# Attention outputs kept feature-major into the output projection, in a two-layer-norm FFN, attention, FFN kernel on one core

## The reference

```python
x = x + 0.5 * ffn(layernorm(x))          # FP4 quantise-dequantise in blocks of 16, gate/up 256 -> 704, down 704 -> 256
x = x + attn(layernorm(x), w_qkv, w_out)
x = x + 0.5 * ffn(layernorm(x))

def attn(x, w_qkv, w_out):               # 16 heads of 16 features
    q, k, v = split(einsum('bte,fe->btf', x, w_qkv))
    weights = softmax(einsum('bihd,bjhd->bhij', q, k) * 16 ** -0.5)
    attn = einsum('bhij,bjhd->bhid', weights, v)
    return einsum('btf,ef->bte', concat(attn over heads), w_out)
```

## Time and profile before

| | |
|---|---|
| median of 3 runs | 4236.52 us (4235.23 to 4238.32) |
| the profiled execution, own time | 4238.47 us |
| span of the profiled execution | 4236.7 us |
| TensorE clock granted, mean | 0.984 |
| busy: PE, DVE, ACT, POOL | 4088.2, 3740.0, 2465.5, 1089.6 us |

### The profile page before, as it was taken

The page is one execution under the profiler, slowest core; times in us unless marked ns, Lnnn a source line. Parts: engine busy times, 40 slices in busy tenths (PEclk is TensorE's granted clock), DMA queues, the critical chain, the costliest instruction groups (busy, mean ns, idle before and its releaser), DMA issues. The chain is left out here.

```text
span 4236.7 us, 109983 instructions
## 1 busy us (share of the span) xinstructions
PE 4088.2 (96%) x46770; PEld 2148.8 (51%) x46770; DVE 3740.0 (88%) x6453; ACT 2465.5 (58%) x2780; POOL 1089.6 (26%) x1190
## 2 busy tenths in 40 slices
PE   3999989889999999999999999999999999899999
PEld 2777765534444444444444444444444443677776
DVE  7999973679999999999999999999999995599998
ACT  1222225457777777777777777777777777222222
POOL 3888863300000000000000000000000000388886
PEclk7999999989999999999999999999999999999999
DMA  2000003300000000000000000000000000000000
GB/s 110 1 1 1 1 1 116 130 24 25 17 24 18 24 18 23 19 22 19 21 21 21 22 19 23 18 24 17 25 17 25 17 25 2 0 11 16 21 16 20
DMA packets 53392, 103.23 MB, mean 24 GB/s; under 512 B 10800, under 2 KB 37808, under 8 KB 52400
## 3 DMA queue, kind: packets, MB, share of 16 engines
q1 hardware_dynamic: 52912, 96.30, 6.8%
HBM read 61.93 MB, written 33.55 MB: 23 GB/s over the span
## 5 line engine op out<-in xcount | busy, mean ns | idle before, releaser
L881 DVE TENSOR_REDUCE mx<-ps_b 128x1 f32<-128x512 f32 x4032 | 2495.8, 682 | 109.8 <-PE ps_b L953 16.9
L868 ACT ACTIVATE probs<-ps_s 128x1024 f32<-128x1024 f32 x2048 | 1984.0, 1021 | 730.1 <-PE ps_s L1000 730.1
L953 PE MATMUL ps_b<-K,Q 96*32 96x512 bf16 x16128 | 1594.3, 381 | 15.5 <-DMA K<-qk_parts_dram 14.0
L1000 PE MATMUL ps_s<-Q,K 99*32 99x512 bf16 x16384 | 1429.0, 379 | 2.4 <-ACT probs L868 2.4
L978 PE MATMUL ps_o<-probs,V 128*32 128x512 f32 x8192 | 1062.3, 591 | 0.4 <-ACT probs L868 0.4
L1000 PEld LDWEIGHTS ps_s<-Q,K 99*32 99x32 bf16 x16384 | 455.2, 97 | 624.8 <-issue 283.8
L953 PEld LDWEIGHTS ps_b<-K,Q 96*32 96x32 bf16 x16128 | 444.7, 96 | 639.0 <-issue 264.7
L499 PE MATMUL ps_gu_f<-w_guT,zT_f 128*128 128x352 f32 x2048 | 635.6, 464 | 10.4 <-DVE h_f L404 9.5
L827 POOL TENSOR_TENSOR neg_parts<-neg_max,zeros 128x16 bf16<-128x16 f32 x64 | 14.2, 222 | 1892.8 <-issue 1793.0
L499 PEld LDWEIGHTS ps_gu_f<-w_guT,zT_f 128*128 128x128 f32 x2048 | 383.3, 192 | 205.4 <-ACT zT_f L356 12.0
L509 PE MATMUL ps_dn_f<-w_dnT,hT_f 128*128 128x256 f32 x1536 | 353.0, 379 | 5.3 <-ACT hT_f L361 5.3
(11 more groups left out here) (116 smaller groups left out, 2624.4 us busy)
## 6 DMA issues: line engine op xcount, KB each, us to landing
qk_parts_dram<-qk_parts SPq DMA_DIRECT2D x96, 256.0 KB, 2.8
Q<-qk_parts_dram SPq DMA_DIRECT2D x64, 192.0 KB
K<-qk_parts_dram SPq DMA_DIRECT2D x64, 192.0 KB
x_res<-in_L_attn_x SPq DMA_DIRECT2D x4, 2048.0 KB, 19.4
Q<-qk_parts_dram SPq DMA_DIRECT2D x64, 128.0 KB
K<-qk_parts_dram SPq DMA_DIRECT2D x64, 128.0 KB
out<-x_res SPq DMA_DIRECT2D x16, 512.0 KB, 2.6
Q<-qk_parts_dram SPq DMA_DIRECT2D x64, 64.0 KB
```

What stands on the lines that cost most here:

```text
L868: nc.scalar.activation(probs[:, (2 * kt + half) % 4, :], ps_s[:, half, :], ACT.Exp, scale=float(DH) ** -0.5).then_inc(exped, 1)
L881: nc.vector.tensor_reduce(mx[:, s, k // 4, bass.ds(k % 4, 1)], ps_b[:, bank, :], AX.X, ALU.max).then_inc(bank_free, 1)
L953: last = nc.tensor.matmul(ps_b[j:j + STRIP, bank, :], Q[s][0:PAIRS, qt * P + j:qt * P + j + STRIP], K[s][0:PAIRS, kb * 512:(kb + 1) * 512] ...
L1000: last = nc.tensor.matmul(ps_s[j:j + STRIP, half, (c % 2) * 512:(c % 2 + 1) * 512], K[s][:, kt * P + j:kt * P + j + STRIP], Q[s][:, c * 51 ...
```

## The change

The output tile `OT` is no longer transposed. After each head SP issues eight DMAs (`store_head`): for each of the four column groups one moves the 16 feature rows to their place in a feature-major array (16 partitions of a group of eight heads, 2048 tokens along the row; the first group into a buffer of its own, group `n` over the V of group `n-1`), and one moves the denominator row, four partitions of 128, into `denom`. After each eighth head (`g % 8 == 0`), DVE inverts the 128x128 denominators at `kt == 6`, and SP stores them to DRAM, waits for that, and issues eight DMAs which each broadcast one head's 2048 inverses over 16 partitions of `factor` (`spread_denominators`). In the next head POOL multiplies the group's 128x2048 outputs by `factor` in four instructions (`scale_group`). The eighth group is finished inside `merge_phase`. The ring has 65 fills per head. ACT's wait before its copy to `OT` is now for the moves of the head before (`out_moved`).

`merge_phase` multiplies the feature-major arrays as the stationary operand directly with `w_outT`, in 32 groups of two tiles over eight PSUM banks; its last eight groups (batch 3) wait for the last scaling. To make room, the FFN weights are stored to DRAM during the first FFN, their SBUF space holds Q and K of slots 1 and 2 during attention, and SP loads them back in `merge_phase`; the V slots lie in the space of `w_qkvT`.

```diff
+GROUP = P // DH
+OUT_MOVES = 8
...
+    def group(self, n):
+        return self.first_group[:] if n == 0 else self.va[:, (n - 1) * S:n * S]
+def store_head(sp, m, g):
+    n, h = g // GROUP, g % GROUP
+    rows = m.group(n)
+    for c in range(4):
+        sp.dma_start(rows[h * DH:(h + 1) * DH, c * 512:(c + 1) * 512], m.OT[32 * c:32 * c + DH, :]).then_inc(m.out_moved, 16)
+        sp.dma_start(m.denom[h * DH + 4 * c:h * DH + 4 * (c + 1), :],
+                     m.OT[32 * c + DH:32 * c + DH + 1, :].rearrange("o (j q) -> o j q", q=P)).then_inc(m.out_moved, 16)
+def spread_denominators(sp, m, n):
+    sp.wait_ge(m.denom_inverted, n + 1)
+    sp.dma_start(m.denom_home.rearrange("h (p q) -> (h p) q", q=P), m.denom[:]).then_inc(m.denom_stored, 16)
+    sp.wait_ge(m.denom_stored, 16 * (n + 1))
+    if n > 0:
+        sp.wait_ge(m.out_scaled, 4 * n)
+    for h in range(GROUP):
+        sp.dma_start(m.factor[h * DH:(h + 1) * DH, :], m.denom_home[h:h + 1, :].broadcast_to([DH, S])).then_inc(m.factor_loaded, 16)
+def invert_denominators(nc, dve, m, n):
+    dve.wait_ge(m.out_moved, (n + 1) * GROUP * OUT_MOVES * 16)
+    nc.vector.reciprocal(m.denom[:], m.denom[:]).then_inc(m.denom_inverted, 1)
+def scale_group(nc, pool, m, n):
+    rows = m.group(n)
+    pool.wait_ge(m.factor_loaded, (n + 1) * GROUP * 16)
+    for c in range(4):
+        part = rows[:, c * 512:(c + 1) * 512]
+        nc.gpsimd.tensor_tensor(part, part, m.factor[:, c * 512:(c + 1) * 512], ALU.mult).then_inc(m.out_scaled, 1)
...
+            @block.sync
+            def _(sp):
+                if out is None:
+                    sp.dma_start(m.w_ffn_home, m.w_ffn[:]).then_inc(stored, 16)
+                    sp.wait_ge(stored, 16)
+                else:
...
-    FILLS = UNITS + 2
+    FILLS = UNITS + 1
     MAX_AT = 11
     NEG_AT = 13
-    OUT_AT = 3
+    INVERT_AT = 6
...
+        slots = m.w_ffn[0:ROWS, :].bitcast(BF16)
+        Q = [m.Q0[:]] + [slots[:, (2 * s - 2) * S:(2 * s - 1) * S] for s in range(1, SLOTS)]
+        K = [m.K0[:]] + [slots[:, (2 * s - 1) * S:2 * s * S] for s in range(1, SLOTS)]
+        V = [m.w_qkvT[:].rearrange("p k f -> p (k f)").rearrange("p (s t c) -> p s t c", s=SLOTS, c=32)[:, s] for s in range(SLOTS)]
...
+                    if known(g, 1):
+                        sp.wait_ge(o_kept, g)
+                        store_head(sp, m, g - 1)
+                    if known(g, 1) and g % GROUP == 0:
+                        spread_denominators(sp, m, g // GROUP - 1)
...
+                    if g > 1 and g % GROUP == 1:
+                        scale_group(nc, pool, m, g // GROUP - 1)
...
-                        act.wait_ge(inv_done, g - 1)
-                    nc.scalar.copy(OT[:], ps_o[:]).then_inc(o_kept, 1)
+                        act.wait_ge(m.out_moved, (g - 1) * OUT_MOVES * 16)
+                    nc.scalar.copy(m.OT[:], ps_o[:]).then_inc(o_kept, 1)
...
-                def normalise(ring, g):
-                    at, bank = ring.next()
-                    o = ps_b[:, bank].rearrange("p (j c d) -> p j c d", j=4, c=4)
-                    dve.wait_ge(bank_full, at + 1)
-                    dve.wait_ge(bank_free, at)
-                    nc.vector.reciprocal(denom[:], o[:, :, :, DH]).then_inc(inv_done, 1)
-                    dve.wait_ge(inv_done, g)
-                    to = m.va.rearrange("p (g c j d) -> p g j c d", c=4, j=4, d=DH)
-                    nc.vector.tensor_tensor(to[:, g - 1], o[:, :, :, 0:DH],
-                                            denom[:].unsqueeze(3).broadcast_to([P, 4, 4, DH]), ALU.mult).then_inc(bank_free, 1)
...
-                        if kt == OUT_AT and known(g, 1):
-                            normalise(ring, g)
+                        if kt == INVERT_AT and known(g, 1) and g % GROUP == 0:
+                            invert_denominators(nc, dve, m, g // GROUP - 1)
...
-                def turn_o(ring, g):
-                    pe.wait_ge(o_kept, g)
-                    bank = take(ring)
-                    for j in range(4):
-                        last = nc.tensor.transpose(ps_b[:, bank, j * P:(j + 1) * P], OT[:, j * P:(j + 1) * P], m.ident[:])
-                    last.then_inc(bank_full, 1)
...
-                        if kt == OUT_AT and known(g, 1):
-                            turn_o(ring, g)
...
+    G = 2
     NG = NT // G
+    BANKS = 8
+    LASTG = B * H // GROUP - 1
+    with ExitStack() as ctx:
+        def sem(name):
+            return ctx.enter_context(nc.semaphore(name))
+        ps_y = ctx.enter_context(nc.psum_tensor("ps_y", [P, BANKS, G, D], F32))
+        y_done, x_done = sem("y_done"), sem("x2_done")
+        w_loaded = sem("ffn_w_back")
+        with nc.Block() as block:
+            @block.sync
+            def _(sp):
+                store_head(sp, m, B * H - 1)
+                sp.dma_start(m.w_ffn[:], m.w_ffn_home).then_inc(w_loaded, 16)
+                spread_denominators(sp, m, LASTG)
+                sp.wait_ge(w_loaded, 16)
+            @block.gpsimd
+            def _(pool):
+                scale_group(nc, pool, m, LASTG)
+            @block.tensor
+            def _(pe):
+                for i in range(NG):
+                    b = i // (NG // B)
+                    if i == (B - 1) * (NG // B):
+                        pe.wait_ge(m.out_scaled, 4 * (LASTG + 1))
+                    if i >= BANKS:
+                        pe.wait_ge(x_done, i - BANKS + 1)
+                    for t in range(G):
+                        tile = (i * G + t) % KT
+                        for k in range(KD):
+                            last = nc.tensor.matmul(ps_y[:, i % BANKS, t, :], m.group(b * KD + k)[:, tile * P:(tile + 1) * P],
+                                                    m.w_outT[:, k, :], start=(k == 0), stop=(k == KD - 1))
+                    last.then_inc(y_done, 1)
+            @block.vector
+            def _(dve):
+                invert_denominators(nc, dve, m, LASTG)
+                for i in range(NG):
+                    dve.wait_ge(y_done, i + 1)
+                    tiles = m.x[:, i * G:(i + 1) * G, :]
+                    nc.vector.tensor_tensor(tiles, ps_y[:, i % BANKS], tiles, ALU.add).then_inc(x_done, 1)
+                    dve.wait_ge(x_done, i + 1)
+                    for t in range(G):
+                        nc.vector.bn_stats(m.stats[:, i * G + t, :], m.x[:, i * G + t, :])
...
+                m.first_group, m.factor = (outs.enter_context(nc.sbuf_tensor(n, [P, S], F32)) for n in ("first_group", "factor"))
+                m.OT = outs.enter_context(nc.sbuf_tensor("OT", [P, 512], F32))
+                m.denom = outs.enter_context(nc.sbuf_tensor("denom", [P, P], F32))
+                m.o_kept, m.out_moved, m.denom_inverted, m.denom_stored, m.factor_loaded, m.out_scaled = (
+                    outs.enter_context(nc.semaphore(n))
+                    for n in ("o_kept", "out_moved", "denom_inverted", "denom_stored", "factor_loaded", "out_scaled"))
+                attend_phase(nc, m)
+                merge_phase(nc, m)
         norm_phase(nc, m, "n3")
```

More of the change, by code:

```diff
@@ L514, in _ @@
                 straight(step)
-            if out is not None:
-                @block.sync
-                def _(sp):
+            @block.sync
[4 more added lines that the diff above has]
+                else:
                     G = 4
@@ L758, in fills_before @@
             if not isinstance(g, int) or g < NH - 1:
-                return g * FILLS + FILLS_AHEAD - (1 if known(g, 1) else 0)
-            return (NH - 1) * FILLS + FILLS_AHEAD - 1 - LEAD + (g - (NH - 1))
+                return g * FILLS + FILLS_AHEAD
+            return g * FILLS + FILLS_AHEAD - LEAD
         def fills_to_neg(n):
@@ L931, in body @@
                             keep_neg(ring, g + 1)
-                heads(dve, body, lambda: normalise(ring_of(NH), NH))
+                heads(dve, body, lambda: None)
             @block.tensor
@@ L1015, in tail @@
                     values(NH - 1, (NH - 1) % SLOTS, KT - 1)
-                    turn_o(ring_of(NH), NH)
                 ahead = Ring(0, 0)
@@ L1048, in body @@
[L1048 to L1055, removed]
-                batches(pool, body)
+                scale_group(nc, pool, m, LASTG)
@@ L1059, in _ @@
             @block.tensor
             def _(pe):
-                def step(i, q, live):
-                    if live(1):
-                        pe.wait_ge(a_ready, i + 2)
-                        if live(-1):
-                            pe.wait_ge(aT_kept, i)
-                        for t in range(G):
-                            flat = a[:, 1 - q, t].rearrange("p h d -> p (h d)")
-                            for k in range(KD):
-                                last = nc.tensor.transpose(ps_T[:, 1 - q, t * KD + k, :], flat[:, k * P:(k + 1) * P], m.ident[:])
-                        last.then_inc(a_turned, 1)
-                    if live(0):
-                        pe.wait_ge(aT_kept, i + 1)
-                        if live(-2):
```

(47 more changed lines are left out.)

17 lines of the change are left out of this document (1 added, 16 removed).

## The result

| | before | changed |
|---|---|---|
| median, us | 4236.54 (4235.23 to 4238.32, 4 runs) | 4175.14 (4172.18 to 4178.28, 4 runs) |
| span of the profiled execution | 4236.7 | 4173.4 |
| forecast | | 4178, range 4168 to 4194 |

The ratio of changed to before is 0.9857, 95% interval 0.9845 to 0.9869: 61 us faster. A second measurement of both gave 4174.86 (4 runs) against 4235.91 (7 runs), ratio 0.9856 (0.9839 to 0.9872).

What follows compares the result with a forecast made beforehand. TensorE was taken to bound attention. Gains of 44.2 (heads) and 17.5 (merge) less 2.5 (denominators), moves at 0, gave 59.2 us off; forecast 4178 us, range 4168 to 4194.

Steps and rivals of the forecast that it cites:

- What bounds: Attention heads: TensorE sets the pace at 2.60 us a `kt` step, against 2.4 us for VectorE's four maxima.
- Term 1: Attention heads: `turn_o` and `normalise` leave, 0.705 us a head in 62 heads plus 0.5 in the last, gain 44.2 us.
- term 3: A group's denominators: 0.95 us reciprocal stalls about 0.4 us in each of seven groups, broadcasts 0; loss 2.5 us.
- Term 2: Eight SyncE moves a head: landed by 2042 at the latest, four microseconds of slack before the inversion, cost 0.
- the fast bound of 2.5: A group's broadcasts: the 1 MB goes at 419 GB/s in 2.5 us and costs nothing.
- Term 4: Merge, last copy to `OT` until the norm: 78.7 us becomes 61.2, gain 17.5 us.
- the rival on the queue: Weights' reload and broadcasts at 58 GB/s hold back the last group; TensorE waits 29 us before batch 3; 4221 us; 5%.

Runs made afterwards that it cites:

- VectorE light: The kernel before with `normalise` cut to its reciprocal, so VectorE does not multiply the outputs into the array; 4235.81 us.
- TensorE light: The kernel before with one transpose in `turn_o` in place of four, `normalise` whole; 4216.28 us.
- the removal alone: The kernel before without `turn_o` and `normalise`, 65 ring fills a head, no output DMAs, merge as before; 4193.29 us, ratio 0.9898.

## Why the prediction was right

The forecast was 4178, the result 4175: the medians moved by 61.4 us where 59.2 were forecast. The mechanism was right, but that the sum came so near is in part luck: attention gave 1.0 us less than forecast (40.7 against 44.2 − 2.5) and the merge 3.5 more, and of those some 2 are the clock's drop in the one execution of before that was profiled. By its steps:

- **What bounds.** Right: TensorE paces attention. VectorE light leaves the time as it was, TensorE light takes 20 us off.
- **Term 1, 44.2 us.** The size was right: 62 steps of 0.705 and 0.70 in the last head are 44.4; the removal alone gave 42.7 between the copies, short by the hundredths named in term 3. The reading of its last tenth was wrong. The 0.11 us beyond the transposes' slot were put down to a wait for a ring bank while VectorE normalises. With VectorE light they stay. They are TensorE's own, before the transposes (0.97 us from `values` to `turn_o` in the earlier trace rows's trace, 0.86 elsewhere), with the bank free for a microsecond.
- **Term 2, moves at nothing.** Right, with 13.9 us to landing and 3.5 us of slack.
- **Term 3, 2.5 us.** 0.94 us for the reciprocal was forecast as 0.95; the stall is 0.22 to 0.25 us a group (1.6 us for seven), not 0.4. The ring forgave 0.7 us, and the forgiveness of 0.57 was got from the misread 0.11. Instead heads run some hundredths over 41.95 in `kt` 6 to 12 (2.605 to 2.610), about 1 to 2 us in 63 heads. These are in the removal alone too, so not from the moves. Nor are they a wait for VectorE: in these steps TensorE fills a ring bank 0.35 to 0.39 us after VectorE freed it, as in steps of 2.60, where at the inversion, when it does wait, that falls to 0.06. Steps of 2.607 and 2.608 stand at `kt` 8 and 9 of the kernel before as well. Their cause stays open. Together 44.4 − 40.7 = 3.7 us against 2.5 (and 44.2). The broadcasts cost 0, as taken, but their 1 MB took about 8 us (133 GB/s over 1232 to 1239), three times the fast bound of 2.5.
- **Term 4, 17.5 us.** Mis-sized: 21 by the profiled pair, about 19 without the drop of the clock in before. From the end of the copy the changed merge takes 57.6 us, not 61.2. 2.0 us of that is the rate: the 57.5 us came from dividing 3.62 by 16 and 7.07 by 32, but a record is 0.38 long and starts 0.216 after the one before, so a run of n lasts (n − 1) × 0.216 + 0.38. The same rows give 0.216 each: (7.07 − 0.38)/31. The 256 take 55.5 us. The other 1.7 us is the clock, which was forecast to be lowered for a while: TensorE stayed at the full level, 2.4 GHz. It waited 0.96 us before its first multiply, where before it waited 2.53 for its first transpose; but that the shorter wait is the reason is not shown, since with VectorE light TensorE waited 2.06 us and stayed at the full level too.

The merge in windows of the changed kernel; the clock column is 1.00 throughout, where in the profiled execution of before it was 0.74 on average over the first 13 us.

```profile
3552.00:3556.00 4.00, 3.87 (x18) 3.46 (x19) 0.00 (x0) 0.00 (x0) 0.00 (x0) 1.00 0.12 28
...
3560.00:3564.00 4.00, 4.00 (x20) 3.54 (x19) 3.90 (x9) 0.00 (x0) 0.00 (x0) 1.00 0.95 404
3564.00:3610.00 46.00, 43.62 (x203) 38.06 (x201) 40.37 (x89) 0.60 (x1) 4.97 (x4) 1.00 0.17 26
```

The weights' reload runs at 404 GB/s, as the rival on the queue had against it, and lands in 9.3 us. The chain ends with the scaling at 3581.5, 29.7 us after the last copy (forecast 27 to 28), and batch 3 is due at 3552.1 + 192 × 0.216 = 3593.6: 12 us of slack where 15 were forecast.

## What to carry to other kernels

Find the pacing engine from the period of one steady instruction, and price a removed piece by how much longer that period is in the steps that hold it: that gave 44 us where 42.7 were measured, even though part of its cause was misread. Look at the same stretch in more than one execution before a difference is put down to the change: the old merge varied by 2 us with the clock. Take the rate of pipelined records from the distance of their starts, not from a run's length divided by its count. Work that moves to DMA and idle engines is free only up to its due time, so write down slack and price: here 3.5 us of slack at the inversion, and missing it costs more than the wait, because TensorE stops and comes back at the lower of its two clock levels.

## What the runs showed of the hardware that was not expected

- One 128x128 f32 transpose among strip matmuls cost TensorE 0.377 us, four cost 0.705, one in bf16 0.28.
- Broadcasting eight 8 KB DRAM rows to 16 partitions each kept all 16 DMA engines busy (share 1.01) at 125 GB/s, 8 GB/s an engine; at a share of 0.2, three engines, the same data went at 61 to 70 GB/s, about 20 GB/s an engine. Five times the engines gave less than twice the rate. Why is not shown: that sixteen engines read the same row at once was not tested apart from their number.
